# A two-layer transformer on one core: layer-0 experts computed for each token's two picks in units of 512 rows, and the layer-1 projection moved behind the gathers

## What is computed

```python
x = _layernorm(x + _L0_attn_ref(...))   # causal softmax attention, 16 heads of 8
x = _layernorm(x + _L0_ffn_ref(...))    # 8 experts, each token weighs its best two
x = _layernorm(x + _L1_attn_ref(...))   # causal attention with a Taylor feature map
x = _layernorm(x + _L1_ffn_ref(...))    # 8 experts, each takes its best 512 tokens
```

```python
logits = x @ router_weight
top_vals, top_idx = jax.lax.top_k(logits, K)            # K = 2
scores = jax.nn.softmax(top_vals, axis=-1)
w = jnp.zeros((T, E), x.dtype).at[jnp.arange(T)[:, None], top_idx].set(scores)
gu = jnp.einsum('th,ehf->tef', x, gate_up_proj) + gate_up_proj_bias
gate, up = jnp.minimum(gu[..., ::2], 7.0), jnp.clip(gu[..., 1::2], -7.0, 7.0)
act = (up + 1.0) * gate * jax.nn.sigmoid(gate * 1.702)
down = jnp.einsum('tei,eih->teh', act, down_proj) + down_proj_bias
out = jnp.einsum('te,teh->th', w, down)
```

## Time and profile before

| | us |
|---|---|
| Median of 3 runs | 874.67 (871.64 to 878.95) |
| Profiled execution, its own time | 872.83 |
| Its span, first to last instruction | 871.1 |
| Busy: PE | 677.3 (78%) |
| Busy: DVE | 560.3 (64%) |
| Busy: POOL | 506.0 (58%) |
| Busy: ACT | 464.6 (53%) |
| Mean granted TensorE clock | 0.900 of full |

### The profile page before, as it was taken

How to read it: one execution, slowest core, us unless ns; L and a number is a source line. 1 busy time by engine, 2 the same in 40 slices (tenths; PEclk the granted TensorE clock), 3 DMA queues, 4 the chain that set the end, 5 groups by cost and what they waited for, 6 DMA issues and landing times. The chain is left out here.

```text
span 871.1 us, 18432 instructions
## 1 busy us (share of the span) xinstructions
PE 677.3 (78%) x6663; PEld 420.5 (48%) x6663; DVE 560.3 (64%) x1476; ACT 464.6 (53%) x690; POOL 506.0 (58%) x652
## 2 busy tenths in 40 slices
PE   7747999999768999999986767999996513898400
PEld 3423555555435566666653434766664202555300
DVE  5877888888377977787787662444546884122116
ACT  5434777777655666666654674667663600232102
POOL 7844777767553555555554784666663602787743
PEclk9976999999989999999997996999998755899765
DMA  5764473431000000000002799999990350355344
GB/s 159 245 212 95 126 192 101 120 85 42 3 2 1 1 2 1 1 1 1 1 2 78 235 287 184 199 194 189 186 196 12 107 137 13 75 122 100 34 88 126
DMA packets 134984, 86.04 MB, mean 99 GB/s; under 512 B 11120, under 2 KB 131440, under 8 KB 134768
## 3 DMA queue, kind: packets, MB, share of 16 engines
q1 hardware_dynamic: 128112, 79.57, 38.6%
q0 software_dynamic: 5632, 4.33, 3.8%
q10 hardware_dynamic: 1152, 0.98, 0.4%
HBM read 54.96 MB, written 29.49 MB: 97 GB/s over the span
## 5 line engine op out<-in xcount | busy, mean ns | idle before, releaser
L771 POOL TENSOR_TENSOR m_prod<-m_upc,m_gatec 128x512 f32<-128x512 f32 x64 | 99.5, 1555 | 101.9 <-DVE m_upc L601 101.9
L2161 ACT ACTIVATE a_prob<-a_ps_pair 128x1024 f32<-128x1024 f32 x96 | 93.1, 1024 | 48.2 <-PE a_ps_pair L1997 36.3
L2173 POOL TENSOR_SCALAR_AFFINE_SELECT a_prob<-a_prob 128x512 f32<-128x512 f32 (+1 forms) x96 | 76.5, 804 | 51.1 <-ACT a_prob L2161 50.9
L1832 ACT ACTIVATE a_prob<-a_ps_pair 128x1024 f32<-128x1024 f32 x96 | 96.6, 1024 | 13.2 <-PE a_ps_pair L1635 10.3
L1873 POOL TENSOR_SCALAR_AFFINE_SELECT a_prob<-a_prob 128x512 f32<-128x512 f32 (+1 forms) x96 | 75.5, 787 | 41.2 <-ACT a_prob L1832 40.5
L1771 DVE TENSOR_REDUCE a_mx<-a_ps_pair 128x4 f32<-128x1024 f32 x64 | 77.8, 1220 | 24.3 <-PE a_ps_pair L1676 22.6
L715 ACT ACTIVATE m_gate<-m_ps_g,bgu 128x512 f32<-128x512 f32 x64 | 44.0, 687 | 47.5 <-PE m_ps_g L460 47.5
L460 PE MATMUL m_ps_g<-m_x1T,wgu 128*128 128x512 f32 x128 | 66.2, 599 | 0.0
L1417 ACT ACTIVATE c_hT<-c_ps_x,c_w 128x512 f32<-128x512 f32 x16 | 11.0, 688 | 102.2 <-PE c_ps_x L1236 102.2
L462 PE MATMUL m_ps_u<-m_x1T,wgu 128*128 128x512 f32 x128 | 65.4, 592 | 0.0
L1450 POOL DMA_INDIRECT sum<-c_o,c_idx x32 | 50.4, 1574 | 16.5 <-issue 8.5
(11 more groups left out here) (297 smaller groups left out, 1696.9 us busy)
## 6 DMA issues: line engine op xcount, KB each, us to landing
qst<-scratch_q SPq DMA_DIRECT2D x64, 128.0 KB, 4.0
kst<-scratch_k SPq DMA_DIRECT2D x64, 128.0 KB, 3.9
scratch_q<-p_parts SPq DMA_DIRECT2D x16, 384.0 KB, 2.8
scratch_k<-p_parts SPq DMA_DIRECT2D x16, 384.0 KB, 2.8
qst<-scratch_q SPq DMA_DIRECT2D x32, 192.0 KB, 5.4
kst<-scratch_k SPq DMA_DIRECT2D x32, 192.0 KB, 5.3
c_w<-in_w SPq DMA_DIRECT2D x8, 578.0 KB, 3.9
scratch_q<-parts SPq DMA_DIRECT2D x16, 256.0 KB, 2.5
```

The lines of the kernel that those rows point to most:

```text
L771: nc.gpsimd.tensor_tensor(prod[:, n % 2, :], upc[:, n % 2, :], gatec[:, n % 2, :], ALU.mult).then_inc(s_pr, 1)
L1832: nc.scalar.activation(prob[:, r % 6, :], pair[(0, 2, 1)[j]][:, :], ACT.Exp, scale=scale, bias=0.0).then_inc(s_e, 1)
L2161: nc.scalar.activation(prob[:, r % 6, :], pair[r % 2][:, :], ACT.Square, scale=scale, bias=1.0).then_inc(s_e, 1)
L2173: nc.gpsimd.affine_select(out=blk, in_=blk, compare_op=ALU.is_ge, fill=0.0, base=0, pattern=[[0, n], [1, P]], channel_multiplier=-1).then_ ...
```

## The change

`expert_layer0` and `project_layer1` become one function and one block, `picked_experts`. The 32 tiles are taken in two halves of 16. For each half:

- DVE finds the two picks of every token (`mark_picks`), two matmuls count them (`prefix`), and DVE turns the counts into a place for each pick (`place_picks`), so that the picks of one expert lie together and each expert begins at a multiple of 512 rows. 4096 picks and at most 511 rows of padding for each of 8 experts give 15 units of 512 rows.
- POOL writes each token's row to its two places in a DRAM tensor, `picked`, by 32 plain indirect DMAs of 128 rows.
- For each unit, SP loads its 512 rows (256 KB), PE transposes them, and the unit goes through the matmuls of its one expert. ACT copies that expert's gate and up weights into a small buffer. Which expert it is, PE and ACT read from SBUF into a register (`value_load`) once a unit. DVE clips straight from PSUM, ACT's sigmoid-shaped gelu gives gate times sigmoid(1.702 gate) in one pass, and DVE multiplies. The bias is added by a matmul. ACT copies the result out of PSUM, and SP stores it to a second DRAM tensor, `downs`.
- POOL gathers the two result rows of each token, eight indirect DMAs of 128 rows for a chunk of 512 tokens, and DVE adds them with their weights to the residual.

There are thus 30 units in place of 64 steps, and POOL's 64 products are gone. Chunks 0 to 2 are combined within the unit loop (at units 21, 24 and 27), chunk 3 behind it, and chunks 4 to 7 inside the loop of the layer-1 projection, each behind its gathers; the projection of chunk `c` stands in front of the combining of chunk `c + 2`. In the projection, the subtractions are now matmuls with a negative identity in bf16 that add into the same PSUM bank (`less_hi`, `less_mid`), and POOL has no part in it. The two DRAM tensors need zeros in the padding: SP writes them in 30 DMAs of 256 KB, one in each of 30 steps of the layer-0 attention, from a tile that POOL clears.

The core of the diff:

```diff
+UNIT = 512
+HALF = NTILE // 2
+NUNIT = (2 * P * HALF + E * (UNIT - 1)) // UNIT
+WX = 2 * P + 4
+XIN, WBUFS, OBUFS, GBUFS = 4, 3, 3, 4
+COMBINE_AT = (21, 24, 27)
...
-                def product(n):
-                    after(pool, s_gl, n - 1)
-                    pool.wait_ge(s_gc, n + 1)
-                    pool.wait_ge(s_ucl, n + 1)
-                    nc.gpsimd.tensor_tensor(prod[:, n % 2, :], upc[:, n % 2, :], gatec[:, n % 2, :], ALU.mult).then_inc(s_pr, 1)
...
-                for n in range(E * NCH):
-                    product(n)
...
-                def lo(c, i):
-                    pool.wait_ge(s_mid, 4 * c + i + 1)
-                    nc.gpsimd.tensor_tensor(part(c, i, 2), resid[:, i, :], part(c, i, 1), ALU.subtract).then_inc(s_lo, 1)
...
+                def load(n):
+                    if n % NUNIT == 0:
+                        sp.wait_ge(s_sc[n // NUNIT], 32 * HALF)
+                    after(sp, s_up, n - XIN + 1)
+                    sp.dma_start(xin[:, n % XIN, :], unit_rows(picked, n)).then_inc(s_xin[n % XIN], 16)
+                def store(n):
+                    sp.wait_ge(s_ob, n + 1)
+                    sp.dma_start(unit_rows(done_d, n), ob[:, n % OBUFS, :]).then_inc(s_ost[n % OBUFS], 16)
+                for n in range(NU2 + XIN - 1):
+                    if n < NU2:
+                        load(n)
+                    if n >= XIN - 1:
+                        store(n - XIN + 1)
...
+                def turn_unit(n):
+                    pe.wait_ge(s_xin[n % XIN], 16 * (n // XIN) + 16)
+                    if n < 2:
+                        pe.wait_ge(s_xT, NCH)
+                    after(pe, s_ux, n - 1)
+                    for j in range(4):
+                        last = nc.tensor.transpose(ps_x[n % 2][:, j * P:(j + 1) * P], xin[:, n % XIN, j * P:(j + 1) * P], ident[:, :])
+                    last.then_inc(s_up, 1)
+                def expand(n):
+                    w = wbuf[:, n % WBUFS, :]
+                    pe.wait_ge(s_ux, n + 1)
...
+                    nc.tensor.matmul(ps_g[n % 2][:, :], w[:, 0:P], xT[:, n % 2, :], start=True, stop=True).then_inc(s_g, 1)
+                    after(pe, s_uc, n - 1)
+                    nc.tensor.matmul(ps_u[n % 2][:, :], w[:, P:2 * P], xT[:, n % 2, :], start=True, stop=True).then_inc(s_u, 1)
+                def reduce(n):
...
+                    after(pe, s_ob, n - 1)
+                    e = pe.value_load(expert[0:1, n:n + 1], min_val=0, max_val=E - 1)
+                    nc.tensor.matmul(ps_d[n % 2][:, :], sel[:, bass.ds(e, 1), :].bitcast(BF16), bdq[:, :, :],
+                                     start=True, stop=False, skip_group_check=True)
+                    pe.wait_ge(s_act, n + 1)
+                    for j in range(4):
+                        here = slice(j * P, (j + 1) * P)
+                        last = nc.tensor.matmul(ps_d[n % 2][:, here], act[:, n % 2, here], wd[:, bass.ds(e, 1), :],
+                                                start=False, stop=True, skip_group_check=True)
+                    last.then_inc(s_dn, 1)
...
+                def less_hi(c, i):
+                    pe.wait_ge(s_hi, 4 * c + i + 1)
+                    nc.tensor.matmul(ps_qk[i][:, :], minus[:, :], part(c, i, 0), start=False, stop=False,
+                                     skip_group_check=True).then_inc(s_r1, 1)
...
+                turn_unit(0)
+                for n in range(NU2):
+                    if n + 1 < NU2:
+                        turn_unit(n + 1)
+                    expand(n)
+                    if n >= 2:
+                        reduce(n - 2)
+                reduce(NU2 - 2)
+                turn_next(0)
+                reduce(NU2 - 1)
+                for c in range(NCH):
...
+                    nc.vector.tensor_scalar(idx[:, :, HALF * h:HALF * h + HALF], place[:, :, :, 0], -1.0, None, ALU.add).then_inc(s_idx, 1)
...
+                def clip_gate(n):
+                    u = n % 2
+                    ve.wait_ge(s_g, n + 1)
+                    after(ve, s_gl, n - 1)
+                    nc.vector.tensor_scalar(gatec[:, u, :], ps_g[u][:, :], wbuf[:, n % WBUFS, 2 * P:2 * P + 1], LIMIT, ALU.add, ALU.min)\
+                        .then_inc(s_gc, 1)
...
+                def activate(n):
+                    u = n % 2
+                    ve.wait_ge(s_gl, n + 1)
+                    ve.wait_ge(s_uc, n + 1)
+                    after(ve, s_dn, n - 1)
+                    nc.vector.scalar_tensor_tensor(act[:, u, :], upc[:, u, :], wbuf[:, n % WBUFS, 2 * P + 3:2 * P + 4], glu[:, u, :],
+                                                   ALU.add, ALU.mult).then_inc(s_act, 1)
+                def add_picks(c):
+                    ve.wait_ge(s_got[c % GBUFS], 128 * (c // GBUFS) + 128)
+                    for k in range(2):
+                        for t in range(4):
+                            after(ve, s_y, 8 * c + t + 1 if k else 0)
+                            y = xn[:, 4 * c + t, :]
+                            nc.vector.scalar_tensor_tensor(y, got[:, c % GBUFS, k, t * P:(t + 1) * P], wk[:, k, 4 * c + t:4 * c + t + 1], y,
+                                                           ALU.mult, ALU.add).then_inc(s_y, 1)
...
+                def lo(c, i):
+                    ve.wait_ge(s_r2, 4 * c + i + 1)
+                    after(ve, s_store[4 * (c % 2) + i], 16 * (c // 2))
+                    nc.vector.tensor_copy(part(c, i, 2), ps_qk[i][:, :]).then_inc(s_lo, 1)
...
+                place_picks(0)
+                mark_picks(1)
...
+                for n in range(NU2):
+                    clip_gate(n)
+                    if n > 0:
+                        activate(n - 1)
+                    clip_up(n)
+                    if n in COMBINE_AT:
+                        add_picks(COMBINE_AT.index(n))
...
+                    if 4 <= c + 2 < NCH:
+                        add_picks(c + 2)
+                        row_stats(c + 2)
+                        merge_rows(c + 2)
+                        invert(c + 2, c + 3)
+                        normalise_next(c + 2)
...
+                    after(act_e, s_u, n - WBUFS + 1)
+                    after(act_e, s_act, n - WBUFS + 1)
+                    e = act_e.value_load(expert[0:1, n:n + 1], min_val=0, max_val=E - 1)
+                    nc.scalar.activation(wbuf[:, n % WBUFS:n % WBUFS + 1, :], wall[:, bass.ds(e, 1), :], ACT.Copy).then_inc(s_wb, 1)
+                def gated(n):
+                    act_e.wait_ge(s_gc, n + 1)
+                    after(act_e, s_act, n - 1)
+                    nc.scalar.activation(glu[:, n % 2, :], gatec[:, n % 2, :], ACT.Gelu_apprx_sigmoid).then_inc(s_gl, 1)
+                def copy_out(n):
+                    act_e.wait_ge(s_dn, n + 1)
+                    after(act_e, s_ost[n % OBUFS], 16 * (n // OBUFS))
+                    nc.scalar.activation(ob[:, n % OBUFS, :], ps_d[n % 2][:, :], ACT.Copy).then_inc(s_ob, 1)
...
+                def mid(c, i):
+                    act_e.wait_ge(s_r1, 4 * c + i + 1)
+                    nc.scalar.activation(part(c, i, 1), ps_qk[i][:, :], ACT.Copy).then_inc(s_mid, 1)
...
+                for n in range(NU2):
+                    if n + 1 < NU2:
+                        copy_unit(n + 1)
+                    gated(n)
+                    if n + WBUFS - 1 < NU2:
+                        take_weights(n + WBUFS - 1)
+                    if n >= 2:
+                        copy_out(n - 2)
+                    if n >= NU2 - 2:
+                        normalise_next(n - NU2 + 2)
...
+                def scatter(h):
+                    pool.wait_ge(s_idx, h + 1)
+                    pool.wait_ge(s_x1, NCH * (h + 1))
+                    pool.wait_ge(s_x1a, NCH // 2 * (h + 1))
+                    pool.wait_ge(s_x1p, NCH // 2 * (h + 1))
+                    for t in range(HALF * h, HALF * h + HALF):
+                        for k in range(2):
+                            nc.gpsimd.indirect_dma_start(out=picked[h], out_offset=bass.IndirectOffsetOnAxis(ap=idx[:, k, t:t + 1], axis=0),
+                                                         in_=xn[:, t, :], in_offset=None, compute_op=ALU.bypass).then_inc(s_sc[h], 16)
+                def gather(c):
+                    after(pool, s_y, 8 * (c - GBUFS) + 8)
+                    for k in range(2):
+                        for t in range(4):
+                            tile = 4 * c + t
+                            nc.gpsimd.indirect_dma_start(out=got[:, c % GBUFS, k, t * P:(t + 1) * P], out_offset=None, in_=done_d[c // 4],
+                                                         in_offset=bass.IndirectOffsetOnAxis(ap=idx[:, k, tile:tile + 1], axis=0))\
+                                .then_inc(s_got[c % GBUFS], 16)
+                def stored(n):
+                    for i in range(OBUFS):
+                        pool.wait_ge(s_ost[i], 16 * len(range(i, n, OBUFS)))
...
+                scatter(0)
+                scatter(1)
```

(12 more changed lines are left out.)

884 lines of the change are left out of this document (395 added, 489 removed).

## The result

The changed kernel takes 1060.91 us (median of 4 runs, 1059.38 to 1061.87) beside 876.25 for the kernel before (871.64 to 878.95): a ratio of 1.211, 95% interval 1.205 to 1.217. The forecast was 989 with a range of 934 to 1066. The direction, the place and the mechanism were right, and the size was 72 us short.

The account below looks back on a forecast made before the run. PE bounds the old expert loop; the new one waits on a ring of copy, store, load and landing, 9.6 us a period. The next attention starts 116.4 us later: 872.83 + 116.4 = 989 us, range 934 to 1066.

Parts of the forecast that it names:

- loads are ahead: Rival for the unit loop: loads come early and PE sets the pace at 3.45 us a unit; 828 us, chance 0.04.
- POOL sets the pace: Rival for the unit loop: no exposed load, but plain scatters cost 1.88 us each; 857 us, chance 0.02.
- The high end: Top of the range: low clock throughout, landings of 3.9, first 32 scatters at 1.88; 1024 + 22 + 20 = 1066 us.
- 0 to 2 us, taken as 0: Layer-0 attention: 30 clears, 7.9 MB beside loads issued ahead, and POOL's clear of the tile cost 0 to 2 us.
- the first scatter can start at 262.0: Routing: stage starts at 243.8, first half's logits at about 252.2, then DVE's operations and two matmuls until 262.0.
- Scatters at 1.25 us: Ahead of the loop: POOL issues 32 scatters at 1.25 us each, 40.0 us, and 2.6 to land, until 304.6.
- First steps, at the low clock: Start of the unit loop: three steps with loads already there, at the low clock, 16.9 us, to 324.5.
- The period, 9.6 between 8.2 and 11.0: Unit loop: 8.2 us a period at full clock, 11.0 at low clock, middle 9.6; 25 periods are 240.0 us.
- The register load, taken as 0.4: Unit loop, on ACT ahead of the weight copy: a register load from SBUF, between nothing and 2.6, taken as 0.4 us.
- the landing: Unit loop: SP's load of 256 KB lands in 3.0 us, with only one store ahead of it.
- the projection of chunks 0 to 6 hides beside the gathers: Behind the loop: gathers of chunks 4 to 7 set the end, then chunk 7's work; 67 us to the next attention.
- No change behind the stage: From the next attention on nothing changes; it starts at 644.7 in place of 528.3, 116.4 us later.

Follow-up runs that it names:

- the fourth edit: Changed kernel with later stores, ACT's order and clears on ACT's queue, plus PE counting the first half's picks ahead of the last two chunks' transposes and logits: 857.40 us.
- when alone: Kernel before with only the 30 clears issued from SP and POOL's clear of their tile: 887.55 us, ratio 1.014 to the kernel before.
- ACT's order: Changed kernel with ACT normalising chunk c + 1 just ahead of its copy in the layer-1 projection: 1125.75 us on chip A, again 1122.21 on chip B.
- all four: Changed kernel with later stores, ACT's order, clears on ACT's queue and early count of picks: 857.40 us on chip C, again 856.41 on chip D, ratio 0.980.
- the later stores alone: Changed kernel with SP's load of unit n behind the store of unit n - 6, not n - 4: 982.89 us on chip A, again 984.18 on B.
- three of them: Changed kernel with later stores, ACT's order and the 30 clears issued from ACT's queue instead of SP's: 956.04 us on chip B, ratio 1.081.

## Why the prediction was right, and where it was short

What bounds the loop was read rightly from the order on SP's queue: load n + 1 behind store n - 3, no load ahead despite four buffers. The rivals "loads are ahead" and "POOL sets the pace" are excluded by the 27 waits. Moving the stores by two units, and nothing else, took off some 150 us on one chip. The step times follow, forecast against trace:

| step | forecast | trace | difference |
|---|---|---|---|
| start of the stage | 243.8 | 258.6 | +14.8 |
| to the first scatter | 18.2 | 27.2 | +9.0 |
| to the first unit's transposes | 45.6 | 44.6 | -1.0 |
| first steps, to unit 4 | 21.1 | 15.3 | -5.8 |
| loop from there to the end of the last reduction | 249.0 | 265.6 | +16.6 |
| tail to the next attention | 67 | 105.8 | +38.8 |
| sum | | | +72.4 |

That 1060.91 lies inside 934 to 1066 owes something to luck. The high end was made of the low clock throughout, landings of 3.9 and first scatters at 1.88, and none of these came in full. What filled the range were the tail, the start of the stage and the routing, 62.6 us together, for which it had no room of its own.

- *Clears, "0 to 2 us, taken as 0"*: mis-sized, 14.8, and 14.1 when alone. I priced bytes and not SP's issue slots, though they stood in my own rows: an issue of 0.33 to 0.66 us, 30 times, is 10 to 20 us on a queue that the stage depends on.
- *Routing, "the first scatter can start at 262.0"*: mis-sized. I priced DVE's operations and not PE's order, in which the first half's count stands behind the logits of the second half. DVE waited 5.9 us for it, where 1.4 was priced; the fourth edit gave back 4.2:

```profile
281.70 0.29 DVE L697 COPY m_tot<-m_ps_u 128x128 f32<-128x128 f32 x1 [5.85 <-PE m_ps_u L528]
```

Most of the rest is the estimate of the first half's logits, 8.4 behind the first normalisation. DVE takes them at 271.58, 13.0 behind it, in a stretch that the first row of the profile after shows at 0.50 of the clock. This was not tried.

- *Scatters at 1.25 us*: right, (366.6 - 285.8) / 63 = 1.28. The end of the range at 1.88 is out.
- *First steps, at the low clock*: the transposes take 0.60 and the gate and up 1.02 each from 335.7 on, the values of the full clock, and the steps took 10.8 in place of 16.9.
- *The period, 9.6 between 8.2 and 11.0*: 10.2 in the timeline, nearer the low clock: the clock averages 0.67, and the gate and up have the low clock's pitch. The rows that the prediction read, could not settle this. From unit 4's transposes to unit 29's it is 10.14 on average, 13.5 of the loop's 16.6. The register load, taken as 0.4, measured 0.28 on ACT and 0.30 on PE, and the landing 2.8 for 3.0; both were minor.
- *Tail, "the projection of chunks 0 to 6 hides beside the gathers"*: this step failed. The last gathers landed at about 656.5 (653.9 and 2.6), 45.2 behind the last reduction and forecast at 46.4, but DVE added the last chunk's rows at 689.2. ACT's normalisation of chunk c + 2 stands ahead of the roundings of chunk c + 1 and waits for DVE, PE for ACT, and DVE for PE, so that the chunks run at 17.4 us, where the forecast had read some 7 from the old projection. These are DVE's adding steps of chunks 5 to 7 and one of ACT's waits:

```profile
654.41 2.18 DVE L746 SCALAR_TENSOR_TENSOR xn<-m_got,m_wk,xn 128x128 f32<-128x128 f32 x8
671.92 2.18 DVE L746 SCALAR_TENSOR_TENSOR xn<-m_got,m_wk,xn 128x128 f32<-128x128 f32 x8
...
678.03 0.88 ACT L883 ACTIVATE xn<-xn,m_shift,m_rstd 128x128 f32<-128x128 f32 x2 [8.43 <-DVE m_shift L764]
...
689.21 2.18 DVE L746 SCALAR_TENSOR_TENSOR xn<-m_got,m_wk,xn 128x128 f32<-128x128 f32 x8
```

32.7 of the tail's 38.8 lie there; the way of the last chunk from DVE's adding to the next attention took 27.9 for 20.6, and the gathers were 1.2 shorter. ACT's order took back 11 to 13. That some of the rest is the serial length of DVE's combining and the projection is read from the timeline and was not tried.

- *No change behind the stage*: right within 1.0 us.

The Trainium skill (DMA: Bandwidth & Descriptors, section Latency and other measured facts) gives a tensor_load a floor of about 0.6 us. This case's register loads from SBUF took half of it, 0.28 and 0.30 in the median of 30 each, so here the measurement decides. The same page's 2.0 us plus the bytes over 436 GB/s (section Anatomy of one DMA — SWDGE (gpsimd) path) gave 2.6 for 256 KB, an estimate. That fit is for DMAs that GpSimd issues, and these loads are SP's; they landed after 2.7 at least and 2.8 in the median.

What stays open: each edit's worth on a chip without rests, where only all four were measured together (857.40, 203.5 us below the changed kernel's first 1060.91, the chip of which is not known). An estimate from the worths above, if they add: 857 + 4.2 + 14 + 11 to 13 is 886 to 888 for the later stores alone, where the expectation of their first run had 890, and they would then be worth some 174 us there.

## What to carry to other kernels

Buffers give no lead by themselves: on an in-order queue the load of a unit must also stand ahead of every store that waits for newer work, and one look at "which unit's store is this load behind" tells whether the period is a ring or an engine's. When work is put into the shadow of another stage, price the issuing queue's slots there and not only the bytes. And in a chain of engines that hand chunks on, an instruction for chunk c + 2 that stands ahead of chunk c + 1's makes the wait of one the wait of all.

## What the hardware showed that was not expected

- On two of four chips ACT and DVE waited for PE's increments long after the matmul's recorded end, up to 33 us at a time with the wait for the first unit left out, while POOL issued 32 indirect DMAs in a row; on the two others such waits were 2.8 us at most, and the first measurement of the changed kernel has none over 1 us in the stage. The changed kernel took 1137.0 on one of the first two and 1060.9 in that measurement, with some 7 us of the difference ahead of the stage. The kernel before, with fewer of these DMAs beside PE's work, took 881 and 885 on the first two chips and 877 and 876 on the others. What delays them was not found, nor whether it is the increment or the matmul itself that is late: that they coincide with POOL's DMAs is seen, and no run took these away on such a chip. A kernel with many indirect DMAs beside a PE loop should be measured on more than one chip: with all four edits it is 2% under the kernel before on chips C and D, with three of them 8% over it on chip B, and all four were not run there.
- The low clock is a cost of the ring itself. PE rested 3.9 us a period and had 0.67 of the clock; with products put into that rest it had 1.00, and the period was 2.4 us shorter with them than without. With the loads ahead the period fell by 6.9 us, from 10.2 to 3.3, of which the rest itself is 3.9 and the passes at the low clock 3.0.
